# A fused adaLN, Mamba and FFN kernel: the unit numbers of its side work are shifted by one to three

## The chip, the cores and the metric

The kernel runs on one core of one Trainium2 chip. The metric is the device time of one execution in microseconds (us); lower is better. The engines are TensorE (PE in the rows), its weight load (PEld), VectorE (DVE), ScalarE (ACT), GpSimd (POOL) and SyncE (SP), which issues the DMAs.

## The reference, cut to what matters

```python
# x: 16 x 512 x 256; mod = silu(c) @ wmod gives six rows of 256 for each of the 16 sequences
h  = layernorm(x) * (1 + ca) + sa
xn = layernorm(h, ln1);  a = mamba1(xn) + flip(mamba2(flip(xn)))
x  = x + ga * (layernorm(a, ln2) + xn)
h  = layernorm(x) * (1 + cb) + sb
h  = silu(h @ w1) * (h @ w2);  h = gelu(h @ h1);  h = gelu(h @ h2);  x = x + gb * (h @ w3)

# mamba, E = 512 channels, N = 64 states each, T = 512 steps
xp, z = split(xn @ W_in);  xc = silu(conv4(xp) + conv_b)
dt_lo, B, C = split(xc @ W_xp);  dt = softplus(dt_lo @ W_dt + dt_b)
for t: s[e, n] = exp(dt[t, e] * A[e, n]) * s[e, n] + dt[t, e] * xc[t, e] * B[t, n]
y[t, e] = sum_n s[e, n] * C[t, n];   out = ((y + xc * D) * silu(z)) @ W_out
```

All of it is float32; the hidden width of the FFN is 1024.

## The kernel before, in words

Both scans of one sequence are cut into 128 units, numbered 0 to 127. A unit is four groups of 32 channels with four states each on the 128 partitions, times 512 steps, in two halves of 128x1024. For each unit ScalarE makes the decays exp(dt*A) (`decays`, L1083, two units ahead), the driving term dt*x*B comes into PSUM (even units: VectorE multiplies, L1272; odd units: ScalarE and GpSimd make a product `v_sb`, L1096 and L1380, which TensorE transposes into `driven`, L883), VectorE scans each half (L1283), GpSimd multiplies by C (L1313), and TensorE sums over the states into `y_ps` (`accumulate`, L905). There are 4 buffers for states, 2 for the driving term, 2 for `v_sb`.

One body handles one sequence. It also carries side work: the FFN of the sequence before (parts "early" and "late"), the second half of this sequence's projections ("p1"), the output projection ("o0"), and norm and projections of the next sequence ("next"). There are 18 bodies: "pre" (side work alone), "first", fourteen "mid", "last" and "tail" (side work alone).

The order is written out by hand. `side_steps` and `projection_steps` give each step a unit number on each engine, from the constants of L49 to L54; in `body`, each engine does its part of a unit and then the side steps that have this number. Each engine runs its program strictly in order; steps are tied by semaphores. A side result in PSUM has one bank per stream: `p_ps` for projections and `q_ps` for the FFN, and a new TensorE step waits until ScalarE (or VectorE) has taken the step before out of the same bank (`bank_free`, L706). TensorE does the transposes for the odd unit u+1 in unit u, and side steps after them; after the side steps of an odd unit u come at once the transposes for unit u+2.

Names of steps: T, X, K (transpose, input projection, convolution by four matmuls), xc (silu over the convolution), BC, CL, BT (the B and C rows, C again with the low-rank dt, B transposed), D0 to D3, exp, one, rest, ln, dt (softplus), ua, ub (dt*x on GpSimd), cut, Z0 to Z3 and sz (gate and its silu); N, F0 to F7, silu, glu, H0 to H7, gelu, G0 to G7, gelu, W (the FFN; H, G take two units each on TensorE); o_, n_, x_, h_ with stats, aggr (VectorE), rstd (GpSimd), norm (ScalarE); x_scale, x_shift (L1231, L1234), mix (L1238), mixed (L1360). On ScalarE the functions exp, silu, gelu and ln are in different tables, so silu, gelu, ln, xc and sz each sit between two table loads. A unit whose number is in `CROWDED` has more than two TensorE side steps in its pair, and does `accumulate` earlier.

Of the kernel before, what the change touches and what calls it, by code (L numbers as in the profile page):

```python
# [11 lines left out]
BATCH, T, D = 16, 512, 256  # L12
# [6 lines left out]
EC = E // P  # L19
# [28 lines left out]

P1_AT, X_AT, NEXT_AT, O0_AT = 12, 64, 80, 68  # L49
PASS_AT, FIRST_PASS_AT = (3, 5, 7, 9), (118, 119, 120, 121)  # L50
O1_AT, MIX_AT, N_AT, PRE_AT = 3, 15, 24, (5, 7, 14)
FFN_AT = (("early", 26, 38, 55, 72), ("late", 77, 89, 106, 123))
UT_AT = (121, 10, 26, 41, 57, 73, 78, 97)
GAPS = {"p1": 3, "next": 3}  # L54


def projection_steps(part, s):

    gap = GAPS[part]
# [12 lines left out]
    act.append((s + 5, part, "BC", 1))  # L72
    dve.append((s + 6, part, "BC", 1))
    pe += [(s + 7, part, "CL", 0), (s + 8, part, "CL", 1)]
    act.append((s + 8, part, "CL", 2))
    pe += [(s + 9, part, "BT", 0), (s + 10, part, "BT", 1)]
    act.append((s + 10, part, "BT", 1))
    for m in range(EC):
        pe.append((s + 11 + m, part, f"D{m}", 1))
        act.append((s + 11 + m, part, f"D{m}", 2))  # L80
    act += [(s + 15, part, "exp", 1), (s + 15, part, "one", 1)]
    dve.append((s + 17, part, "rest", 2))
    act.append((s + 18, part, "ln", 1))
    dve += [(s + 19, part, "dt", 1), (s + 22, part, "cut", 1)]
    pool = [(s + 20, part, "ua", 1), (s + 21, part, "ub", 1)]
    for m in range(EC):
        pe.append((s + 22 + m, part, f"Z{m}", 1))
        act.append((s + 22 + m, part, f"Z{m}", 1))
    act.append((s + 26, part, "sz", 1))
    return pe, act, dve, pool  # L90


def norm_steps(part, name, s):

    dve = [(s, part, name + "_stats", TT), (s + 1, part, name + "_aggr", TT)]
    if name == "x":
        dve += [(s + 4, part, "x_scale", 1), (s + 5, part, "x_shift", 1)]
    return [(s + 2, part, name + "_rstd", 9)], [(s + 3, part, name + "_norm", TT)], dve


def side_steps():
# [113 lines left out]
def adaln_kernel(nc, x, win, wxp, wdt, wout, f1, h1, h2, w3, cols, rows, c_t, wmod, consts, spread_rows, out):  # L215
    ctx = ExitStack()
    with ctx:
# [239 lines left out]
        def _(sp):  # L457
# [166 lines left out]
            def body(at):  # L624
                for unit in range(UNITS):
# [821 lines left out]
```

## Time and profile before

| | us |
|---|---|
| median of three runs | 12745.45 (12720.19 to 12750.62) |
| the profiled execution | 12767.88, span 12766.1 |
| VectorE busy | 11968.4 (94%) |
| GpSimd busy | 11345.7 (89%) |
| ScalarE busy | 10843.4 (85%) |
| TensorE busy | 10393.6 (81%) |

The span is setup and the body "pre" up to 168 us, sixteen bodies with scans up to 12509 us, and the tail of 257 us. Busy time is the union of an engine's instructions; the idle time printed behind an instruction is that of its engine just before it, with the instruction that ended it. A row of the timeline merges equal instructions that follow each other. The scans of the body that the rows are taken from (the sixth with scans) begin at 4032.7 us and those of the next one at 4799.5 us, so this body is 766.7 us long.

### The profile page before, as it was taken

The page shows a single profiled execution, that of the slowest core. Times are in us where ns is not written, and L with a number is a line of the kernel's source. Part 1 is how long each engine was busy: PE and PEld are TensorE (multiplying, and loading weights), DVE is VectorE, ACT ScalarE, POOL GpSimd, SP SyncE. Part 2 cuts the span into 40 slices and gives each one's busy share as a digit, 9 for nine tenths or more (in the row PEclk, how much of TensorE's full clock was granted, in tenths as well). Part 3 has the DMA queues.
Part 4 walks back from the last instruction along what each step waited for, and adds up shares of the span by engine and source line. Part 5 has one row for each costly group of instructions (what it writes and reads, how often), then busy time and mean ns, then how long its engine had stood idle before and what let it go on. Part 6 is the DMA issues. An engine that isn't in the chain of part 4 may idle for free.

```text
span 12766.1 us, 179504 instructions
## 1 busy us (share of the span) xinstructions
PE 10393.6 (81%) x51484; PEld 5920.3 (46%) x51484; DVE 11968.4 (94%) x7080; ACT 10843.4 (85%) x23460; POOL 11345.7 (89%) x5924
## 2 busy tenths in 40 slices
PE   5678878888888888878888888887878878788887
PEld 2334544445454444544445444454544445444445
DVE  5999999999999999999999999999999999999992
ACT  5788888888888898888888888888888988888882
POOL 4899999899998999999998998999989999999992
PEclk7778988889898998988989898998989989889888
DMA  2223333333333333433333333333333333333332
GB/s 89 83 87 111 119 112 126 122 108 117 110 127 115 117 125 106 130 111 121 122 113 115 112 125 121 109 120 107 128 111 119 123 108 127 112 124 121 111 111 96
DMA packets 610266, 1459.04 MB, mean 114 GB/s; under 512 B 68928, under 2 KB 110032, under 8 KB 604672
## 3 DMA queue, kind: packets, MB, share of 16 engines
q1 hardware_dynamic: 609152, 1446.18, 35.0%
q8 instruction: 456, 7.47, 0.2%
q14 instruction: 658, 5.39, 0.1%
HBM read 1355.09 MB, written 90.83 MB: 113 GB/s over the span
## 4 chain that ended last, share of the span: by engine, by line
issue 26%; PE 25%; ACT 19%; DVE 16%; POOL 10%; DMA 1%; DVEq 0%; POOLq 0%; SPq 0%; ACTq 0%
DVE state L1283 11%; POOL state L1313 8%; PE driven L883 7%; ACT state L1083 7%; ACT v_sb L1096 6%; PE q_ps L838 5%; PE y_ps L905 4%; DVE driven L1272 3%; PE p_ps L746 2%; PE q_ps L825 2%; PE b_ps L873 1%; PE p_ps L754 1%; ACT L1083 1%; PE p_ps L770 1%; PE p_ps L761 1%
## 5 line engine op out<-in xcount | busy, mean ns | idle before, releaser
L1313 POOL TENSOR_TENSOR state<-state,c_rep 128x1024 f32<-128x1024 f32 x4096 | 9682.4, 2393 | 971.5 <-DVE state L1283 965.2
L1283 DVE TENSOR_TENSOR_SCAN state<-state,driven 128x1024 f32<-128x1024 f32 x4096 | 9089.4, 2267 | 298.0 <-PE driven L883 280.5
L1083 ACT ACTIVATE state<-ud_rep,cols_sb 128x512 f32<-128x512 f32 x8192 | 5212.5, 710 | 3.1 <-PE y_ps L905 0.6
L1096 ACT ACTIVATE v_sb<-u_t,b_t 128x128 f32<-128x128 f32 x12288 | 4062.0, 505 | 1136.5 <-PE driven L883 1133.4
L883 PE MATMUL driven<-consts_sb,v_sb 128*128 128x128 f32 x16384 | 2713.9, 320 | 1486.3 <-DVE state L1283 1463.2
L883 PEld LDWEIGHTS driven<-consts_sb,v_sb 128*128 128x128 f32 x16384 | 2184.5, 164 | 2692.0 <-DVE state L1283 2001.2
L905 PE MATMUL y_ps<-state,consts_sb 128*32 128x512 f32 x16384 | 2455.2, 677 | 289.2 <-POOL state L1313 287.1
L1272 DVE TENSOR_TENSOR driven<-ud_rep,b_ps 128x1024 f32<-128x1024 f32 x2048 | 2389.6, 1212 | 18.1 <-DMA ud_rep<-ud_rows 18.1
L838 PE MATMUL q_ps<-hid,wq_sb 128*128 128x256 f32 x7936 | 2081.0, 408 | 139.8 <-ACT hid L1061 76.4
L838 PEld LDWEIGHTS q_ps<-hid,wq_sb 128*128 128x128 f32 x7936 | 1498.0, 199 | 1016.3 <-issue 818.1
L1380 POOL TENSOR_TENSOR v_sb<-u_t,b_t 128x512 f32<-128x512 f32 x1024 | 1083.5, 1058 | 36.4 <-issue 23.5
L905 PEld LDWEIGHTS y_ps<-state,consts_sb 128*32 128x32 f32 x16384 | 346.6, 114 | 1213.9 <-POOL state L1313 675.2
L873 PE MATMUL b_ps<-b_parts,onehot 32*128 32x512 f32 x1024 | 574.2, 561 | 0.0
L825 PE MATMUL q_ps<-xn_q,wq_sb 128*128 128x256 f32 x1984 | 508.6, 400 | 44.9 <-ACT hid L1051 22.4
L746 PE MATMUL p_ps<-x_t,wp_sb 128*128 128x512 f32 x1024 | 503.6, 615 | 37.3 <-ACT xc L989 24.2
L754 PE MATMUL p_ps<-u_pad,dt_sb 128*128 128x512 f32 x1024 | 514.3, 626 | 20.0 <-ACT u_pad L985 19.9
L825 PEld LDWEIGHTS q_ps<-xn_q,wq_sb 128*128 128x128 f32 x1984 | 365.8, 194 | 221.1 <-issue 99.2
L848 PE MATMUL q_ps<-wq_sb,hid 128*128 128x256 f32 x992 | 282.0, 434 | 68.3 <-ACT hid L1066 64.6
L1061 ACT ACTIVATE hid<-q_ps,cols_sb 128x256 f32<-128x256 f32 x496 | 223.4, 450 | 129.7 <-PE q_ps L838 129.5
L746 PEld LDWEIGHTS p_ps<-x_t,wp_sb 128*128 128x128 f32 x1024 | 189.3, 194 | 269.9 <-issue 185.0
L754 PEld LDWEIGHTS p_ps<-u_pad,dt_sb 128*128 128x128 f32 x1024 | 188.1, 197 | 269.2 <-issue 213.7
L873 PEld LDWEIGHTS b_ps<-b_parts,onehot 32*128 32x128 f32 x1024 | 208.5, 204 | 210.4 <-issue 210.4
(141 smaller groups left out, 5585.8 us busy)
## 6 DMA issues: line engine op xcount, KB each, us to landing
c_rep<-bc_rows SPq DMA_DIRECT2D x2048, 256.0 KB, 3.0
ud_rep<-ud_rows SPq DMA_DIRECT2D x512, 512.0 KB, 4.0
wq_sb<-in_h SPq DMA_DIRECT2D x512, 512.0 KB, 3.9
wq_sb<-in_f SPq DMA_DIRECT2D x128, 512.0 KB, 4.2
wp_sb<-in_win SPq DMA_DIRECT2D x64, 512.0 KB, 4.1
dt_sb<-conv_taps SPq DMA_DIRECT2D x32, 1024.0 KB, 5.2
ud_rows<-u_pad SPq DMA_DIRECT2D x128, 256.0 KB, 3.4
ud_rows<-dt_sb SPq DMA_DIRECT2D x128, 256.0 KB, 3.5
```

Source lines behind the costliest of these rows:

```text
L746: mm = pe.matmul(p_ps[:], wp_sb[:, m, k, :], x_t[:, k, :], start=(k == 0), stop=(k == DC - 1))
L825: mm = pe.matmul(bank[:, which * TH:(which + 1) * TH], w[:, m % 2, which, k, :], n_t[:, k, i * TH:(i + 1) * TH], start=(k == 0), stop=(k = ...
L838: mm = pe.matmul(bank[:, 0:TH], w[:, k, :], src[:, k, :], start=(k == 0), stop=(k == HC - 1))
L873: pe.matmul(b_ps[:], onehot[k, g % quarter, :], b_parts[d][k, :], start=True, stop=True).then_inc(b_spread, 1)
L883: mm = pe.transpose(driven[:, q % DRIVE_RING, j % 2, tt * P:(tt + 1) * P], v_sb[:, unit // 2 % V_RING, tt, j].rearrange("p e n -> p (e n)" ...
L905: mm = pe.matmul(y_ps[EG * j:EG * (j + 1), :], over_nn, state[:, k % STATE_RING, j, :], start=False, stop=(g == NG - 1))
L1083: ins = act.activation(state[:, unit % STATE_RING, j, :], ud_rep[:, nth % 2, j, 1, :], ACT.Exp, scale=a_neg[:, d, c, j, g:g + 1])
L1096: ins = act.activation(v_sb[:, unit // 2 % V_RING, tt, :, :, n].rearrange("p j e -> p (j e)"), u_t[:, nth % 2, tt, :], ACT.Identity, scale ...
L1272: dve.tensor_tensor(driven[:, h], u_rows(unit)[:, 2 * h:2 * h + 2], b_ps[:].unsqueeze(1).to_broadcast([P, 2, T]), ALU.mult).then_inc(dve_d ...
L1283: dve.tensor_tensor_scan(flat, flat, driven[:, q % DRIVE_RING].rearrange("p j t -> p (j t)"), 0.0, ALU.mult, ALU.add).then_inc(scanned, 1)
L1313: pool.tensor_tensor(part, part, c_rep[:, unit % ROW_RING, :].unsqueeze(1).to_broadcast([P, 2, T]), ALU.mult).then_inc(was_read, 1)
L1380: pool.tensor_tensor(v_sb[:, unit // 2 % V_RING, TT - 1].rearrange("p j e n -> p (j e) n"), u_t[:, nth % 2, TT - 1, :].unsqueeze(2).to_bro ...
```

## The change

Steps keep their work and their order within each chain; the unit numbers change. The projections of p1 start two units earlier and those of next three earlier; within a projection everything from BC (on VectorE) and CL on comes one unit later relative to its start, rest two, dt, ua, ub, cut and Z three. So in absolute units, before and after: silu of the FFN 34 to 31 and 85 to 83; first gelu 54 to 51 and 105 to 103; second gelu 71 to 69 and 122 to 121; H starts 38 to 35 and 89 to 87; G starts 55 to 53 and 106 to 105; W 72 to 70, and 123 stays. xc 26 to 24 and 94 to 91; D0 34 to 33 and 102 to 100; exp and one 38 to 37 and 106 to 104; rest 40 stays and 108 to 107; dt 42 to 43 and 110 stays; Z0 45 to 46 and 113 stays; sz 49 to 50 and 117 stays. mix goes from 15 to 12, x_norm from 67 to 65, x_scale from 68 to 67. Loads and stores that belong to these steps move with them.

```diff
-P1_AT, X_AT, NEXT_AT, O0_AT = 12, 64, 80, 68
+P1_AT, X_AT, NEXT_AT, O0_AT = 10, 62, 77, 68
-O1_AT, MIX_AT, N_AT, PRE_AT = 3, 15, 24, (5, 7, 14)
-FFN_AT = (("early", 26, 38, 55, 72), ("late", 77, 89, 106, 123))
-UT_AT = (121, 10, 26, 41, 57, 73, 78, 97)
+O1_AT, O_AT, MIX_AT, N_AT, PRE_AT = 3, 7, 12, 21, (5, 7, 10)
+FFN_AT = (("early", 23, 35, 53, 70), ("late", 75, 87, 105, 123))
+UT_AT = (121, 8, 24, 41, 57, 73, 78, 95)
...
-    dve.append((s + 6, part, "BC", 1))
-    pe += [(s + 7, part, "CL", 0), (s + 8, part, "CL", 1)]
-    act.append((s + 8, part, "CL", 2))
-    pe += [(s + 9, part, "BT", 0), (s + 10, part, "BT", 1)]
-    act.append((s + 10, part, "BT", 1))
+    dve.append((s + 7, part, "BC", 1))
+    pe += [(s + 8, part, "CL", 0), (s + 9, part, "CL", 1)]
+    act.append((s + 9, part, "CL", 2))
+    pe += [(s + 10, part, "BT", 0), (s + 11, part, "BT", 1)]
+    act.append((s + 11, part, "BT", 1))
     for m in range(EC):
-        pe.append((s + 11 + m, part, f"D{m}", 1))
-        act.append((s + 11 + m, part, f"D{m}", 2))
-    act += [(s + 15, part, "exp", 1), (s + 15, part, "one", 1)]
-    dve.append((s + 17, part, "rest", 2))
-    act.append((s + 18, part, "ln", 1))
-    dve += [(s + 19, part, "dt", 1), (s + 22, part, "cut", 1)]
-    pool = [(s + 20, part, "ua", 1), (s + 21, part, "ub", 1)]
+        pe.append((s + 12 + m, part, f"D{m}", 1))
+        act.append((s + 12 + m, part, f"D{m}", 2))
+    act += [(s + 16, part, "exp", 1), (s + 16, part, "one", 1)]
+    dve.append((s + 19, part, "rest", 2))
+    act.append((s + 20, part, "ln", 1))
+    dve += [(s + 22, part, "dt", 1), (s + 25, part, "cut", 1)]
+    pool = [(s + 23, part, "ua", 1), (s + 24, part, "ub", 1)]
     for m in range(EC):
-        pe.append((s + 22 + m, part, f"Z{m}", 1))
-        act.append((s + 22 + m, part, f"Z{m}", 1))
-    act.append((s + 26, part, "sz", 1))
+        pe.append((s + 25 + m, part, f"Z{m}", 1))
+        act.append((s + 25 + m, part, f"Z{m}", 1))
+    act.append((s + 29, part, "sz", 1))
...
-        dve += [(s + 4, part, "x_scale", 1), (s + 5, part, "x_shift", 1)]
+        dve += [(s + 5, part, "x_scale", 1), (s + 6, part, "x_shift", 1)]
...
-    for part, name, s in (("early", "o", MIX_AT - 7), ("early", "n", MIX_AT + 3), ("next", "x", X_AT), ("next", "h", X_AT + 7)):
+    for part, name, s in (("early", "o", O_AT), ("early", "n", MIX_AT + 3), ("next", "x", X_AT), ("next", "h", X_AT + 8)):
```

## Rows read from the trace of the kernel before

**Rows 1.** The page's first part: busy time of each engine.

```profile
PE 10393.6 (81%) x51484; PEld 5920.3 (46%) x51484; DVE 11968.4 (94%) x7080; ACT 10843.4 (85%) x23460; POOL 11345.7 (89%) x5924
```

**Rows 2.** Waits of VectorE over the span: total, times, longest, in us.

```profile
DVE state L1283 <- PE driven L883: 280.5, 373, 3.2
```

**Rows 3.** Waits of VectorE in one body, 4033 to 4799 us.

```profile
DVE state L1283 <- PE driven L883: 13.5, 20, 2.0
DVE state L1283 <- ACT state L1083: 2.6, 1, 2.6
...
DVE xa L1231 <- ACT xa L968: 1.1, 1, 1.1
```

**Rows 4.** Waits of VectorE in units 26 to 40 of that body, 4186 to 4283 us.

```profile
DVE state L1283 <- PE driven L883: 3.4, 5, 1.8
DVE b_parts L1249 <- ACT b_parts L997: 2.1, 1, 2.1
```

**Rows 5.** Timeline of TensorE, unit 35: start, us, instruction, [idle before, releaser].

```profile
4248.07 2.07 PE L791 MATMUL p_ps<-sz 16*128 16x512 f32 x2 [4.38 <-ACT u_pad L1015]
4250.07 1.97 PE L883 MATMUL driven<-consts_sb,v_sb 128*128 128x128 f32 x8
```

**Rows 6.** Timeline of ScalarE, units 34 and 35.

```profile
4238.64 2.55 ACT L1083 ACTIVATE state<-ud_rep,cols_sb 128x512 f32<-128x512 f32 x4
4241.09 2.56 ACT L1096 ACTIVATE v_sb<-u_t,b_t 128x128 f32<-128x128 f32 x8
4243.66 1.28 ACT L1055 ACT_TABLE_LOAD   x1
...
4246.77 0.67 ACT L1014 ACTIVATE dt_sb<-p_ps,cols_sb 128x512 f32<-128x512 f32 x1
...
4249.33 2.56 ACT L1083 ACTIVATE state<-ud_rep,cols_sb 128x512 f32<-128x512 f32 x4
```

**Rows 7.** Timeline of TensorE, units 55 to 57.

```profile
4370.75 3.78 PE L838 MATMUL q_ps<-hid,wq_sb 128*128 128x256 f32 x8 [3.31 <-ACT hid L1066]
4374.32 1.92 PE L883 MATMUL driven<-consts_sb,v_sb 128*128 128x128 f32 x8
...
4377.35 1.09 PE L883 MATMUL driven<-consts_sb,v_sb 128*128 128x128 f32 x8
...
4378.80 1.99 PE L838 MATMUL q_ps<-hid,wq_sb 128*128 128x256 f32 x8
```

**Rows 8.** Timeline of TensorE, units 123 and 124.

```profile
4776.52 3.38 PE L848 MATMUL q_ps<-wq_sb,hid 128*128 128x256 f32 x8 [4.84 <-ACT hid L1066]
```

**Rows 9.** Timeline of VectorE, unit 125.

```profile
4780.82 4.46 DVE L1283 TENSOR_TENSOR_SCAN state<-state,driven 128x1024 f32<-128x1024 f32 x2 [1.95 <-PE driven L883]
```

**Rows 10.** Timeline of VectorE, units 106 to 110.

```profile
4662.31 6.63 DVE L1283 TENSOR_TENSOR_SCAN state<-state,driven 128x1024 f32<-128x1024 f32 x3
...
4680.77 2.29 DVE L1253 SCALAR_TENSOR_TENSOR u_pad<-sz,u_pad 128x2048 f32<-128x2048 f32 x1 [2.60 <-ACT sz L1021]
...
4697.19 4.02 DVE L1259 TENSOR_TENSOR dt_sb<-dt_sb,sz 128x2048 f32<-128x2048 f32 x1 [0.80 <-ACT sz L1024]
```

**Rows 11.** Timeline of ScalarE, the steps exp and one and what follows.

```profile
4676.79 1.92 ACT L1018 ACTIVATE u_pad<-u_pad 128x2048 f32<-128x2048 f32 x1
...
4680.65 2.54 ACT L1083 ACTIVATE state<-ud_rep,cols_sb 128x512 f32<-128x512 f32 x4
```

**Rows 12.** Timeline of VectorE, the second half of rest in unit 40.

```profile
4277.96 4.34 DVE L1255 TENSOR_TENSOR dt_sb<-dt_sb,u_pad 128x2048 f32<-128x2048 f32 x1
```

**Rows 13.** Groups of VectorE by line over the span: the step mix.

```profile
L1238 DVE TENSOR_TENSOR o_sb<-o_sb,mod_q 128x1024 f32<-128x1024 f32 x16 | 85.0, 5312 | 5.6 <-ACT o_sb L968 5.6
```

**Rows 14.** Timeline of VectorE, units 118 and 119 and the drive of 120.

```profile
4741.49 8.81 DVE L1283 TENSOR_TENSOR_SCAN state<-state,driven 128x1024 f32<-128x1024 f32 x4
4750.22 2.34 DVE L1272 TENSOR_TENSOR driven<-ud_rep,b_ps 128x1024 f32<-128x1024 f32 x2
```

**Rows 15.** Timeline of ScalarE, the start of unit 118.

```profile
4750.06 2.56 ACT L1083 ACTIVATE state<-ud_rep,cols_sb 128x512 f32<-128x512 f32 x4
```

More of the change, by code:

```diff
@@ L636, in body @@
                         load_pass(at, unit // NG + 1, PASS_AT.index(unit % NG))
-                    if unit == P1_AT + 11 + 3 * GAPS["p1"] and at.has("p1"):
+                    if unit == P1_AT + 12 + 3 * GAPS["p1"] and at.has("p1"):
                         store_bc(at, "p1")
-                    if 0 <= unit - P1_AT - 3 * GAPS["p1"] - 25 < EC and at.has("p1"):
-                        store_ud(at, "p1", unit - P1_AT - 3 * GAPS["p1"] - 25)
-                    if unit == NEXT_AT + 11 + 3 * GAPS["next"] and at.has("next"):
+                    if 0 <= unit - P1_AT - 3 * GAPS["p1"] - 28 < EC and at.has("p1"):
+                        store_ud(at, "p1", unit - P1_AT - 3 * GAPS["p1"] - 28)
+                    if unit == NEXT_AT + 12 + 3 * GAPS["next"] and at.has("next"):
                         store_bc(at, "next")
-                    if 0 <= unit - NEXT_AT - 3 * GAPS["next"] - 25 < EC and at.has("next"):
-                        store_ud(at, "next", unit - NEXT_AT - 3 * GAPS["next"] - 25)
+                    if 0 <= unit - NEXT_AT - 3 * GAPS["next"] - 28 < EC and at.has("next"):
+                        store_ud(at, "next", unit - NEXT_AT - 3 * GAPS["next"] - 28)
                     if unit in FIRST_PASS_AT and at.has("next"):
@@ L660, in body @@
                         load_wxp(at, "next")
-                    if unit == P1_AT + 28 + 3 * GAPS["p1"] and at.has("o0"):
+                    if unit == P1_AT + 31 + 3 * GAPS["p1"] and at.has("o0"):
                         load_wout(at)
```

## The prediction

> **What bounds the kernel now.** I read the busy times first, then the waits of VectorE over the span and in one body, then the timelines of VectorE, TensorE and ScalarE around each of its waits. VectorE is busy 11968.4 of 12766.1 us [rows 1]. Four scans and their two drives make a pair of units: 8.73 us from the first scan to the drives and about 2.25 for these, 10.97 in all, so 4.37 for an even unit and 6.60 for an odd one [rows 14]. The change removes nothing from that; what it can win is VectorE's waits and what its side operations lose. Waits in one body come to 23.5 us of 766.7: 13.5 for TensorE's transposes, 2.6 for the decays, 2.6 for exp and one, 2.1 for BC, 1.1 for x_norm, 0.8 for ln [rows 3, 4, 10] and 0.8 in small pieces. Over the span the first of them is 280.5 us, 17.5 for each of the 16 bodies [rows 2], so this body is a light one, and I scale its TensorE waits by 17.5/13.5 = 1.3.
>
> How such a wait arises is to be seen at the silu of unit 34. ScalarE begins the unit's decays at 4238.64, the product at 4241.09, the silu's table load at 4243.66, and reads D0 out of its bank from 4246.77; it begins unit 35 at 4249.33 [rows 6]. TensorE stands in unit 35 before D1, which wants that bank, for 4.38 us, and then runs the transposes for unit 37 in 1.97 instead of 1.09 us [rows 5, 7]; VectorE waits 1.8 [rows 4]. The first gelu is the same (idle 3.31, then a step of 3.78 instead of 1.99 [rows 7]), and so is the second late gelu (idle 4.84, VectorE waits 1.95 [rows 8, 9]). Two quantities decide: how far ScalarE is behind when the bank is read, and whether the blocked TensorE step has an odd number. After an odd unit's side steps the transposes come at once. TensorE has 10.97 us from the start of odd unit u to the start of u+2, and the transposes take the last 1.1. A blocked step of 2.0 has to start by 7.9 after VectorE began unit u.
>
> ScalarE's cost of a unit, start to start: 2.45 for decays, 2.4 more in even units (4.8 in all), 1.2 in odd ones (3.65), from rows 6 and the short product of four in odd units, which I take as half of the eight. A function of its own with two table loads is 3.1 to its end [rows 6] and 1.28 more, 4.4. Its lag behind VectorE at the start of a unit is the lag at the unit before, plus its cost there, less VectorE's 4.37 or 6.60. At unit 118 it is 4750.06 - 4741.49 = 8.6 us, right after sz [rows 14, 15].
>
> **The change part by part.** All terms are per body.
>
> *Units 23 to 41.* Now VectorE waits 3.4 + 2.1 here [rows 4], scaled 4.4 + 2.1 = 6.5. BC on VectorE gets a unit more behind ScalarE's BC, 4.4 to 6.6 us against a wait of 2.1: gone. After the silu at 31 come BT (two TensorE steps that wait for nothing of it) and D0 in odd unit 33, which waits for BT's reading in ScalarE's unit 32. With a lag of 8.3 (like after sz), less 0.2 or so for the Y step, that is 8.0 after VectorE's 33: D0 takes 1.0, so no wait at full speed and about 1 at half speed. The pairs of units with four long TensorE steps fall from three to one here. I leave 1.7 (0.5 to 3.5): **-4.8**.
>
> *First gelu, early.* G0 gets a free unit, and the wait (1.7, scaled 2.2) goes. But sz moves to unit 50 and the gelu to 51, two functions of 4.4 us side by side. Lag: 8.2 at 51 (as behind the other sz), 8.2 + 3.65 + 4.4 - 6.60 = 9.7 at 52, 10.1 at 53; the decays of unit 55 (first half 1.3 us after ScalarE's 53 starts) are then there at 11.4 against 10.97: 0.4 of wait. G1 in odd unit 55 waits for G0's reading until 7.5: no wait at full speed, 2.2 at half speed. Between them: 1.7 left, **-0.5**.
>
> *Second gelu, late.* It moves from 122 to 121 and W1 stays at 123: the wait of 1.95, scaled 2.5, goes. But G steps now start in odd units. G6 is read in ScalarE's unit 118, straight after sz in 117: lag 8.2 (the 8.6 of rows 15 less one reading), plus 4.8 for the unit and 0.35 for the reading, less 4.37: 8.95 after VectorE's unit 119, where G7 stands. G7 takes 2.0 and the transposes 1.04: 1.0 late at full speed, 3.4 if it takes the 3.78 and 1.92 of rows 7. Idle before it would be 5 us, longer than in any of rows 5, 7 and 8. I take 2.8: **+0.3**.
>
> *xc of next.* It moves from even 94, where H2 was read before it, to odd 91, and H2 is read behind it in 92. The same arithmetic with a lag of 8.3 gives 9.1 after VectorE's 93, where H3 and half of BC stand, 3.7 us: 2.9 late. The silu at 83 does the same to X2 in 85, one step, 0.4 to 3 late, of which GpSimd's backlog behind glu (which holds TensorE back here now) would have cost most anyway. **+2.9** (0 to +5).
>
> *exp, one, rest, ln, dt of next.* VectorE waits 2.60 for one, 0.80 for ln [rows 10]; both go with one more unit of distance. ScalarE's lag behind gelu, D3, exp and one is 4680.65 (its unit 107) less 4666.7 (VectorE's 107: three scans begin at 4662.31, two of them 4.37) = 13.9 [rows 10, 11]. Today VectorE has rest to do (and waits) in 108 before it needs those decays. After the change rest is in 107, three units behind exp and not two: ScalarE is 13.9 late at 105, the first decays of 107 are there 15.2 after VectorE's 105, and it needs them after 10.97. A new wait of 4.3 for the decays, which takes the place of the old one. And rest: in unit 40, without a wait ahead, its second half takes 4.34 [rows 12], against 2.29 for the first after a wait [rows 10]: a GpSimd operation comes between. In 107 I expect a short one, +1.3 (0 to 2.3); dt, which now starts at once after the scans, loses 1.4 of its 4.02. Sum -2.6 - 0.8 - 0.3 + 4.3 + 1.3 - 1.4 = **+0.5** (-3 to +3).
>
> The Trainium skill, SBUF — State Buffer, section Who interferes with whom, says that a VectorE instruction with two SBUF inputs and a GpSimd one that reads SBUF shut each other out for the whole instruction, by order of issue. By that rule, the trace agrees: 4.34 is 2.29 and most of one GpSimd operation.
>
> *x_norm, x_scale, x_shift.* The wait of 1.1 goes [rows 3]; x_scale then starts straight behind the drives with GpSimd busy, which costs it 0 to 2.1, the difference in rest; I take 0.9: **-0.2**. *mix* takes 5.3 on average [rows 13] and stays among GpSimd's operations, as rstd and pre2 now follow each other: **0** (-2 to +2). BC at 28, ua, ub and Z one later, loads: **+0.5** for the pairs 46 to 49, now both of four long steps. The DMAs move with their steps, each still a unit or more ahead of its reader: 0. Pre and tail keep their order on every engine: 0. The 2.6 at the start of a body stays.
>
> Sum: -4.8 - 0.5 + 0.3 + 2.9 + 0.5 - 0.2 + 0 + 0.5 = -1.3 per body, times 16 (first and last carry part of the steps) -21 us. On the profiled 12767.9 that is 12747. The median stands 22 lower than the profiled run, so **12725**.
>
> The Trainium skill, ScalarE: Activation LUTs, section What ACT_TABLE_LOAD costs, adds a drain of 1.38 us to each load. The trace differs: the load starts 0.01 behind the product before it [rows 6], and no term here has a drain.
>
> **The rivals.** A, *faster*: ScalarE is a little less behind, and the steps in 93 and 119 are not blocked past the limit. For it: both exceed it by 1 us or so at full speed, and each lag is my estimate. Against: the half speed after idling. It takes away 2.9 and 2.8: -7.0 per body, -112, 12633.
>
> B, *slower*: TensorE's half speed follows each new idle stretch. The rows show it behind 3.31, 4.38 and 4.84 us [rows 5, 7, 8]: about the double of 1.99 and 1.09, as at the lower of the clock's two levels (1.2 and 2.4 GHz). At 33, 55, 85, 93 and 119 a step of 2.0 and the transposes take 2.6 longer; 13 in all, of which about 6 are in the sum: +5.7 net, +91 over 16, 12836. [...]
>
> C, *slower*: GpSimd's operations come between mix, x_scale, x_shift, rest and dt more often: 5 of them at 2.05 (4.34 - 2.29) less the 2.2 counted and the 1.4 taken off for dt is +9.4, but not all meet one; half of that is +4.7, net +3.4: 12799.
>
> D, *it does nothing*: all silu and gelu waits only move to the next odd unit, body by body the same 23.5: 12745. That is near my forecast, and held with it.
>
> **How the numbers follow.** Forecast with D 0.40; A 0.33; B 0.17; C 0.10. A measurement of this kernel can tell about 0.3% (38 us) from no change, so faster is below 12707, slower above 12784. Faster: A and a little of the forecast's spread, 0.38. Slower: B and most of C, 0.24. Same: 0.38. The single terms go from -6 to +5 per body, which together give about 4 per body, 65 us, around 12725; the range goes to A below and B above, 12620 to 12840.
>
> **What would show it.** Right: VectorE's wait for BC near 0, its wait for one at L1253 gone, and a new wait of the scans for the decays of 3 to 5 us per body near unit 107; TensorE idle before H3 (unit 93) and before G7 (119) and VectorE waiting behind it; no wait at 125. Wrong: no wait for the decays at 107 (then ScalarE's lag is overrated and A holds), or idle TensorE at 33, 55 and 85 followed by half speed (B), or x_scale and rest above 4 us each (C).

## The result and the profile after

The changed kernel takes 12817.7 us (median, 12814.4 to 12819.0) against 12746.6 for the kernel before: ratio 1.006, 95% interval 1.0042 to 1.0077. It is slower by 71 us. The forecast was 12725, 21 us less than before; the measured time lies inside the range, but it moved the other way, and it ends 18 us from rival B's 12836.

The profiled execution has a span of 12814.7 us, 48.6 more than before. Its busy times, to be held against [rows 1]:

```profile
PE 10278.8 (80%) x51484; PEld 5854.4 (46%) x51484; DVE 11913.4 (93%) x7080; ACT 10888.8 (85%) x23460; POOL 11417.0 (89%) x5924
```

VectorE is busy 55 us less than before, and the span is 49 longer: it waits 104 us more. The waits of VectorE over the span (total us, times, longest):

```profile
DVE state L1283 <- PE driven L883: 359.3, 305, 5.7
DVE state L1283 <- ACT state L1083: 87.9, 44, 4.3
```

The first answers to [rows 2], 280.5 us there in 373 pieces: fewer waits, but longer ones. The second was 10.2. The same in one body, 4045 to 4823 us, against [rows 3]:

```profile
DVE state L1283 <- PE driven L883: 24.2, 18, 4.0
DVE state L1283 <- ACT state L1083: 6.2, 3, 4.3
DVE xc L1202 <- PE y_ps L905: 1.6, 2, 1.4
DVE dt_sb L1262 <- POOL u_pad L1368: 1.1, 1, 1.1
```

The waits for u_pad (exp and one), b_parts, xa and dt_sb <- ACT of [rows 3, 4, 10] are gone from the body, as forecast: 6.6 us. In their place stand 10.7 more for TensorE's transposes and 3.6 more for the decays.

What TensorE waited for shows it best: three of its groups over the span, busy us, mean ns | idle before them, and by whom ended. These are of the kernel before:

```profile
L838 PE MATMUL q_ps<-hid,wq_sb 128*128 128x256 f32 x7936 | 2081.0, 408 | 139.8 <-ACT hid L1061 76.4 <-ACT hid L1066 53.9 <-POOL hid L1364 8.9
L825 PE MATMUL q_ps<-xn_q,wq_sb 128*128 128x256 f32 x1984 | 508.6, 400 | 44.9 <-ACT hid L1051 22.4 <-DMA wq_sb<-in_f 21.4 <-ACT xn_q L1042 0.9
L746 PE MATMUL p_ps<-x_t,wp_sb 128*128 128x512 f32 x1024 | 503.6, 615 | 37.3 <-ACT xc L989 24.2 <-ACT sz L1029 10.8 <-ACT u_pad L1015 1.4
```

and these of the changed one:

```profile
L838 PE MATMUL q_ps<-hid,wq_sb 128*128 128x256 f32 x7936 | 2048.9, 403 | 316.6 <-ACT hid L1061 301.7 <-POOL hid L1364 8.9 <-ACT hid L1066 5.4
L825 PE MATMUL q_ps<-xn_q,wq_sb 128*128 128x256 f32 x1984 | 534.1, 416 | 92.8 <-ACT hid L1051 53.3 <-DMA wq_sb<-in_f 37.7 <-ACT xn_q L1042 0.9
L746 PE MATMUL p_ps<-x_t,wp_sb 128*128 128x512 f32 x1024 | 532.1, 645 | 76.3 <-ACT xc L989 63.4 <-ACT sz L1029 10.6 <-ACT u_pad L1015 1.4
```

L838 are the steps H and G, L825 the steps F, L746 the steps X and Z. L1066 is gelu itself: the free unit behind it works, 53.9 us fall to 5.4. L1061, L1051 and L989 are the short copies with which ScalarE empties TensorE's bank. The waits for those rise by 225, 31 and 39 us. The functions' time has not gone; it stands ahead of the next copy.

By stretches of units, the mean of bodies 1 to 14 in us, worked out from the starts of the first scans of the units in the two traces, against the terms of the sum:

| units | forecast | measured | what it is |
|---|---|---|---|
| 0-19 | 0 | -2.4 | mix -3.4, a new wait of 0.9 at 15 |
| 20-41 | -4.8 | -0.4 | BC gone; new waits 2.1 at 31, 2.3 + 1.4 at 35 |
| 42-49 | +0.5 | +1.0 | cut waits 1.1 for GpSimd's ub |
| 50-57 | -0.5 | +0.4 | decays 1.9 at 54 and 55 in place of 2.0 at 57 |
| 58-73 | -0.2 | -2.1 | x_norm's wait and small ones gone |
| 74-81 | 0 | +4.7 | 3.5 at 77, 1.4 at 80 |
| 82-91 | 0 | +1.9 | 3.7 at 87, less 2.2 at 91 |
| 92-103 | +2.9 | +1.8 | 3.4 at 95, less small ones |
| 104-115 | +0.5 | -0.3 | 4.2 for the decays at 107 in place of 2.6 + 0.8 |
| 116-127 | +0.3 | -0.5 | 3.0 at 121 in place of 2.7 at 125 |
| sum | -1.3 | +4.0 | |

4.0 in each of 14 bodies is 56 us; the first and last body and what lies around them give 7 back.

In the names of the FFN's steps the first digit is 0 for early and 1 for late: H13 is the prediction's H3, G17 its G7, and F06 is the seventh F step of early.

A mean over the bodies hides one thing. One and the same step, behind the same idle time, runs at full speed in some bodies of one execution and wholly or partly at half speed in others. F06 in unit 29 with the step behind it, in the body from 4045 us and in the one from 5601, both of the changed kernel:

```profile
4221.67 2.85 PE L825 MATMUL q_ps<-xn_q,wq_sb 128*128 128x256 f32 x8 [2.12 <-ACT hid L1051]
4224.31 2.76 PE L761 MATMUL p_ps<-xc,sz 128*80 128x512 f32 x4
...
5776.85 1.99 PE L825 MATMUL q_ps<-xn_q,wq_sb 128*128 128x256 f32 x8 [2.13 <-ACT hid L1051]
5778.67 1.88 PE L761 MATMUL p_ps<-xc,sz 128*80 128x512 f32 x4
```

The granted clock is 0.66 from 4222 to 4227 us and 1.00 from 5777.7 to 5782.6. VectorE's wait at unit 31 is 2.4 us behind the first pair and 0.7 behind the second. It is 2.4 in 11 of the 14 bodies here, and in 0 to 8 of 14 in the other kernels with these units. H13 in unit 93, in the body from 4045 us and in the next:

```profile
4616.39 1.99 PE L838 MATMUL q_ps<-hid,wq_sb 128*128 128x256 f32 x8 [3.07 <-ACT hid L1061]
...
5392.22 2.62 PE L838 MATMUL q_ps<-hid,wq_sb 128*128 128x256 f32 x8 [3.07 <-ACT hid L1061]
```

The wait at 95 is 2.9 behind the first kind, in 11 bodies, and 4.6 to 5.7 behind the second, in three. In the kernel before, the wait at 91 is 1.4 or 3.0 in the same way, behind an H step of 1.99 or of 3.5 to 3.7 us in unit 89. So a difference of about 1 us per body between two kernels at 31, 91 or 95 can come from the number of bodies at half speed, with no edit near it; below such differences are named. No run tests what chooses between the two.

### The profile page after: what moved, and what is told of

Read it like the earlier page. It is cut to its first block, busy times and chain, and to the rows that moved or that the text cites. A ratio compares the mean times of both kernels' runs of the same rounds, so it can differ in the third digit from the quotient of the medians.

```text
span 12814.7 us, 179504 instructions
## 1 busy us (share of the span) xinstructions
PE 10278.8 (80%) x51484; PEld 5854.4 (46%) x51484; DVE 11913.4 (93%) x7080; ACT 10888.8 (85%) x23460; POOL 11417.0 (89%) x5924
## 4 chain that ended last, share of the span: by engine, by line
PE 26%; issue 23%; ACT 22%; DVE 14%; POOL 11%; DMA 1%; DVEq 0%; SPq 0%; POOLq 0%; ACTq 0%
DVE state L1283 10%; POOL state L1313 9%; ACT state L1083 8%; PE driven L883 8%; ACT v_sb L1096 7%; PE q_ps L838 5%; PE y_ps L905 4%; DVE driven L1272 3%; PE p_ps L746 2%; PE q_ps L825 2%; ACT L1083 1%; PE b_ps L873 1%; PE p_ps L754 1%; DMA wq_sb<-in_f 1%; PE p_ps L761 1%
## 5 line engine op out<-in xcount | busy, mean ns | idle before, releaser
L883 PE MATMUL driven<-consts_sb,v_sb 128*128 128x128 f32 x16384 | 2655.7, 316 | 1473.3 <-DVE state L1283 1456.6
L883 PEld LDWEIGHTS driven<-consts_sb,v_sb 128*128 128x128 f32 x16384 | 2152.9, 162 | 2696.3 <-DVE state L1283 1893.9
L838 PE MATMUL q_ps<-hid,wq_sb 128*128 128x256 f32 x7936 | 2048.9, 403 | 316.6 <-ACT hid L1061 301.7
L838 PEld LDWEIGHTS q_ps<-hid,wq_sb 128*128 128x128 f32 x7936 | 1473.5, 195 | 1209.0 <-issue 1007.4
L1380 POOL TENSOR_TENSOR v_sb<-u_t,b_t 128x512 f32<-128x512 f32 x1024 | 1151.2, 1124 | 36.2 <-issue 23.1
L825 PE MATMUL q_ps<-xn_q,wq_sb 128*128 128x256 f32 x1984 | 534.1, 416 | 92.8 <-ACT hid L1051 53.3
L746 PE MATMUL p_ps<-x_t,wp_sb 128*128 128x512 f32 x1024 | 532.1, 645 | 76.3 <-ACT xc L989 63.4
L825 PEld LDWEIGHTS q_ps<-xn_q,wq_sb 128*128 128x128 f32 x1984 | 381.3, 202 | 287.0 <-issue 156.5
L1061 ACT ACTIVATE hid<-q_ps,cols_sb 128x256 f32<-128x256 f32 x496 | 226.1, 456 | 130.8 <-PE q_ps L838 130.6
L746 PEld LDWEIGHTS p_ps<-x_t,wp_sb 128*128 128x128 f32 x1024 | 198.9, 203 | 300.8 <-issue 190.4
L1051 ACT ACTIVATE hid<-q_ps,cols_sb 128x256 f32<-128x256 f32 x496 | 202.4, 462 | 99.2 <-PE q_ps L825 99.1
```

Source lines behind the costliest of these rows:

```text
L746: mm = pe.matmul(p_ps[:], wp_sb[:, m, k, :], x_t[:, k, :], start=(k == 0), stop=(k == DC - 1))
L825: mm = pe.matmul(bank[:, which * TH:(which + 1) * TH], w[:, m % 2, which, k, :], n_t[:, k, i * TH:(i + 1) * TH], start=(k == 0), stop=(k = ...
L838: mm = pe.matmul(bank[:, 0:TH], w[:, k, :], src[:, k, :], start=(k == 0), stop=(k == HC - 1))
L883: mm = pe.transpose(driven[:, q % DRIVE_RING, j % 2, tt * P:(tt + 1) * P], v_sb[:, unit // 2 % V_RING, tt, j].rearrange("p e n -> p (e n)" ...
L1380: pool.tensor_tensor(v_sb[:, unit // 2 % V_RING, TT - 1].rearrange("p j e n -> p (j e) n"), u_t[:, nth % 2, TT - 1, :].unsqueeze(2).to_bro ...
```

## The experiments

Ratios are to the kernel before, with their 95% interval; waits are means per body over bodies 1 to 14.

### Which half loses, and what mix is worth

The part of mix alone, on the kernel before:

```diff
-O1_AT, MIX_AT, N_AT, PRE_AT = 3, 15, 24, (5, 7, 14)
+O1_AT, O_AT, MIX_AT, N_AT, PRE_AT = 3, 7, 12, 24, (5, 7, 10)
...
-    for part, name, s in (("early", "o", MIX_AT - 7), ("early", "n", MIX_AT + 3), ("next", "x", X_AT), ("next", "h", X_AT + 7)):
+    for part, name, s in (("early", "o", O_AT), ("early", "n", MIX_AT + 3), ("next", "x", X_AT), ("next", "h", X_AT + 7)):
```

> The kernel before with one part of the change alone: the attention norm at 7, mix at 12, pre2 at 10, the norm n behind mix; all else as before. Theory: mix takes 5.6 us in unit 15 because GpSimd operations that are queued there come before it (pre2 at 14 and a backlog of products); at 12 it takes 2.2, as in the changed kernel. That is -3.4 per body, -54 over 16 bodies: 12692, ratio 0.9958. Rival: the gain of mix belongs to its new neighbours in the changed kernel (projection started two units earlier), here it stays at 5 us: 12746, ratio 1.000.

Measured: 12716.3, ratio 0.9974 (0.9962 to 0.9985). The group of mix in this kernel, against [rows 13]:

```profile
L1238 DVE TENSOR_TENSOR o_sb<-o_sb,mod_q 128x1024 f32<-128x1024 f32 x16 | 31.6, 1977 | 5.6 <-ACT o_sb L968 5.6
```

2.0 us and not 5.3, so the gain needs nothing else of the change; the changed kernel has 2114 ns in the same group. The bodies are 3.3 shorter on average. The run moves mix, the norm o and pre2 together and does not tell which of GpSimd's operations cost mix its time. (The Trainium skill, SBUF — State Buffer, section Who interferes with whom, lets a VectorE instruction with two SBUF inputs and a reading GpSimd one shut each other out by order of issue; a mix of 5.3 us at one place and 2.0 at another agrees with that.) From one profiled execution to the other the span fell by 55 us, as forecast, but the median by 30: the profiled execution of the kernel before stands 21 us above its median, this one 3 below. No row tells where the typical execution loses the rest.

Units 62 to 127 as before, the rest changed:

```diff
-P1_AT, X_AT, NEXT_AT, O0_AT = 10, 62, 77, 68
+P1_AT, X_AT, NEXT_AT, O0_AT = 10, 64, 80, 68
-FFN_AT = (("early", 23, 35, 53, 70), ("late", 75, 87, 105, 123))
+FFN_AT = (("early", 23, 35, 53, 70), ("late", 77, 89, 106, 123))
...
+    w = 1 if part == "p1" else 0
...
+    act += [(s + 15 + w, part, "exp", 1), (s + 15 + w, part, "one", 1)]
+    dve.append((s + 17 + 2 * w, part, "rest", 2))
```

> The changed kernel with units 62 to 127 as before (norms at 64 and 71, projection of next at 80 with the old distances, late FFN at 77, 89, 106, UT7 at 97); the early half stays changed. Theory: the early half is worth -1.5 per body (mix -3.4, BC and first gelu gone, new stalls at 31 and 35) and the late half is the loser: waits at 77, 80, 87, 95, 107 and 121 vanish, those of before at 91, 108 and 125 return: -5.6 per body, 12817 - 84 = 12733, ratio 0.999. Rival: the early half is the loser by its stalls in 31 and 35 and mix gains nothing lasting: ratio above 1.003, 12785 or more.

Measured: 12677.2, ratio 0.995 (0.9934 to 0.9967). The early half of the change makes the kernel faster by 69 us, and the late half costs 140 on top of it, not the 84 that were forecast. In its trace the waits of VectorE for TensorE are 222.8 us, and TensorE's group L838 waits 163.7 and not 316.6. The theory's split was right in its main point, that the late half is the loser; the early half won 69 us and not 24. Part of the difference is the clock and not the order of work: the wait at 31 is 0.7 in all 14 bodies, where the changed kernel has 2.4 in 11, and the waits that came back at 91 and 125 are 1.4 and 1.8, where the kernel before has means of 2.2 and 2.7.

### The wait at unit 77: a load that passed another

The forecast had nothing here. TensorE in the changed kernel, unit 76 on (start, us, instruction, [idle before, releaser]):

```profile
4502.45 1.90 PE L905 MATMUL y_ps<-state,consts_sb 128*32 128x512 f32 x8 [3.13 <-POOL state L1313]
4506.75 3.78 PE L825 MATMUL q_ps<-xn_q,wq_sb 128*128 128x256 f32 x8 [2.40 <-DMA wq_sb<-in_f]
4510.32 1.91 PE L883 MATMUL driven<-consts_sb,v_sb 128*128 128x128 f32 x8
```

F10 waits for its weights, and the DMA queue says why. The queue in the changed kernel, and below it in the kernel before:

```profile
4498.12 0.51 SPq L511 DMA_DIRECT2D dt_sb<-conv_taps  x1
4498.82 0.81 SPq L543 DMA_DIRECT2D wq_sb<-in_f  x2
```

```profile
4496.94 0.80 SPq L543 DMA_DIRECT2D wq_sb<-in_f  x2
4500.16 0.54 SPq L553 DMA_DIRECT2D c_rep<-bc_rows  x1
4500.84 0.50 SPq L511 DMA_DIRECT2D dt_sb<-conv_taps  x1
```

The load of the convolution taps (1 MB) hangs on NEXT_AT, which moved by three units; the chunks of F hang on the late FFN, which moved by two. Both stood in unit 76, chunks first; now the taps are in 73 and the chunks in 74, behind them. The edit puts them into one unit again:

```diff
-                    if unit == NEXT_AT - 4 and at.has("next"):
+                    if unit == NEXT_AT - 3 and at.has("next"):
                         load_conv(at, "next")
```

> The changed kernel with the load of next's convolution taps (1 MB) one unit later in the DMA queue, so that the first two weight chunks of the late FFN are issued ahead of it in unit 74 and not behind it. Theory: TensorE's wait of 2.4 us for the first chunk before step F10 and the half-speed step behind it are from this order; VectorE's wait at unit 77 falls from 3.5 to at most 1, and the 1.35 at unit 80 to about 0.8: -3 per body, -45 over 15 bodies: 12772, ratio to the kernel before 1.002. Rival: the accumulate in unit 76 that waits for GpSimd (3.1 us idle) sets it, not the DMA: the wait at 77 stays at 3 or more, 12817, ratio 1.0056.

Measured: 12755.7, ratio 1.0002 (0.999 to 1.0014). The same steps in this kernel:

```profile
4474.02 1.93 PE L905 MATMUL y_ps<-state,consts_sb 128*32 128x512 f32 x8 [3.13 <-POOL state L1313]
4475.88 2.67 PE L825 MATMUL q_ps<-xn_q,wq_sb 128*128 128x256 f32 x8
4478.39 1.04 PE L883 MATMUL driven<-consts_sb,v_sb 128*128 128x128 f32 x8
```

The idle time for GpSimd is the same 3.13, the one for the DMA is gone, and VectorE's wait at 77 goes from 3.5 to 0.25. So the rival falls. One line of the queue's order is worth 62 us, nearly the whole loss. Not all of it is in unit 77: 1.0 less at 31 and 1.4 more at 95 came with it. The steps there and the idle time before them are the same; half speed stands at 31 in 3 bodies and not in 11, and at 95 in 11 and not in 3. Together the two all but cancel out.

### The steps behind a function

Three waits come from a step of TensorE in an odd unit that needs a bank which ScalarE empties only behind a function. First sz, one unit later:

```diff
-    act.append((s + 29, part, "sz", 1))
+    act.append((s + (29 if part == "p1" else 30), part, "sz", 1))
```

> The changed kernel with one function one unit later: the silu of z for next in 118, behind G16's reading, not in 117 ahead of it. Theory: the step G17 in odd unit 119 waits for G16's reading only because that stands behind sz; VectorE's wait of 3.0 at unit 121 falls below 0.5: -2.7 per body, -41: 12777, ratio 1.0024. Rival: the block moves to the next reading: G17 is read in 120 behind sz and gelu at 121 comes late, so a wait of 2 to 3 us appears at 123 or 125: 12817, ratio 1.0056.

Measured: 12765.7, ratio 1.0012 (0.9998 to 1.0027). G17 in the changed kernel stood idle and was slow:

```profile
4778.22 3.02 PE L838 MATMUL q_ps<-hid,wq_sb 128*128 128x256 f32 x8 [4.11 <-ACT hid L1061]
4781.03 1.73 PE L883 MATMUL driven<-consts_sb,v_sb 128*128 128x128 f32 x8
```

With sz behind the reading, the 3.0 at 121 are gone and nothing of over 0.2 follows up to 125. The theory holds. The 52 us are 11 more than forecast; the wait at 31 is 1.1 lower (half speed in 2 bodies), which this edit does not touch, and the one at 95 0.6 higher.

Then xc from 91 to 92 and BC one later. UT7 (TensorE transposes dt*x of the eighth pass into the same bank, ScalarE copies it out) goes to 96, or BC and UT7 lock each other out:

```diff
-    act.append((s + 3, part, "xc", 1))
+    w = 1 if part == "next" else 0
+    act.append((s + 3 + w, part, "xc", 1))
...
-UT_AT = (121, 8, 24, 41, 57, 73, 78, 95)
+UT_AT = (121, 8, 24, 41, 57, 73, 78, 96)
```

> The changed kernel with the silu xc of next in unit 92, behind H12's reading, and BC (TensorE 93 and 94, ScalarE 94, VectorE 96) and UT7 (96) one later with it. Theory: H13 in odd unit 93 waited only because H12's reading stood behind xc, so VectorE's wait at unit 95 (3.4 us in the changed kernel) falls to about 0.5 (BC's first half in 93 still waits a little for xc): -2.9 per body, -44: 12774, ratio 1.0022; the wait of 4.2 for the decays at 107 stays. Rival: the block moves with xc, BC in 93 now waits for it in full, and the wait at 95 stays at 3 or more: 12817, ratio 1.0056.

Measured: 12776.7, ratio 1.0027 (1.0016 to 1.0038). The wait at 95 is gone, 3.4 to below 0.1, but 1.7 came back at 99. The time was as forecast, 12774, but with luck: without the 1.0 less at 31 (half speed in 3 bodies and not in 11) it would have been about 16 us more.

X2 and what follows one later as well:

```diff
-        x = s + 2 + gap * m
+        x = s + 2 + gap * m + (1 if part == "next" and m > 1 else 0)
```

> As the run with xc in 92, and X2, K2, X3, K3 of next each one unit later, so that the odd unit 85 behind the silu of 83 has no step that waits for a reading (X2 stands in even 86). Theory: the 3.7 us at unit 87 are X2's wait for K1's reading behind that silu, and the half-speed step and transposes behind the idle time; they fall below 0.7: together with xc -6 per body, -90: 12727, ratio 0.9985. Rival: GpSimd's backlog behind the two glu products in 84 and 85 sets the accumulate and the transposes there anyway (that wait was 2.2 at unit 91 in the kernel before): 2 us or more stay at 87, 12750 or more, ratio 1.0003.

Measured: 12807.0, ratio 1.0049 (1.0032 to 1.0066), 80 us above the forecast. The 3.7 at 87 fell to 1.3, so they did belong to X2; but in small pieces all of it returned: 1.3 at 89 to 93 (two long steps in each pair of units there), 0.8 more at 99, 1.5 more at 112, where the Y step (VectorE's product of the summed y, L1202) waits for TensorE. Neither theory holds: below 0.7 or 2 us and more had been forecast for unit 87.

D0 to D3 of p1 one later:

```diff
-        pe.append((s + 12 + m, part, f"D{m}", 1))
-        act.append((s + 12 + m, part, f"D{m}", 2))
+        d = s + 12 + m + (1 if part == "p1" else 0)
+        pe.append((d, part, f"D{m}", 1))
+        act.append((d, part, f"D{m}", 2))
```

> The changed kernel with D0 to D3 of p1 one unit later (34 to 37), so that the odd unit 33 behind the silu of 31 has no step. Theory: D0 in 33 waited for BT's reading behind the silu and then ran at half speed; VectorE's waits at 35 (2.3 + 1.4) vanish: -3.2 per body over 16 bodies, -50: 12767, ratio 1.0016. Rival: the four-step units 35 and 37 (D1 with H00, D3 with H01) and exp and one straight behind D3's reading bring a wait of 2 or more at 37 or for the decays at 39: ratio 1.004 or more.

Measured: 12790.6, ratio 1.0037 (1.0023 to 1.0051), 24 us above the forecast. The first wait at 35 is gone, 0.9 of the second is left, and 2.2 stand at 37: the rival's wait at its place, if with a little less of a loss. TensorE there:

```profile
4239.53 1.94 PE L906 MATMUL y_ps<-state,consts_sb 128*32 128x512 f32 x8 [2.44 <-POOL state L1314]
4241.40 3.78 PE L839 MATMUL q_ps<-hid,wq_sb 128*128 128x256 f32 x8
4245.11 1.42 PE L792 MATMUL p_ps<-sz 16*128 16x512 f32 x2
```

No step waits for a bank here. The first H step takes 3.78 us and not 1.99, behind 2.44 us of idle time for GpSimd's product and an `accumulate` of 1.94.

### Lateness or half speed

At 85 and 33 of the changed kernel, X2 and D0:

```profile
4568.56 3.78 PE L746 MATMUL p_ps<-x_t,wp_sb 128*128 128x512 f32 x4 [4.36 <-ACT xc L989]
4572.13 1.91 PE L883 MATMUL driven<-consts_sb,v_sb 128*128 128x128 f32 x8
...
4249.05 2.07 PE L791 MATMUL p_ps<-sz 16*128 16x512 f32 x2 [4.57 <-ACT b_t L1006]
4251.05 1.97 PE L883 MATMUL driven<-consts_sb,v_sb 128*128 128x128 f32 x8
4252.95 1.94 PE L905 MATMUL y_ps<-state,consts_sb 128*32 128x512 f32 x8
4254.81 1.97 PE L883 MATMUL driven<-consts_sb,v_sb 128*128 128x128 f32 x8
```

The table of stretches has the granted clock (stretch, us, TensorE's busy time, clock, DMA share, GB/s), first with the idle time, then X2:

```profile
4562.00:4568.00 6.00, 2.20 (x11) 0.95 0.15 44
4568.00:4574.00 6.00, 5.44 (x16) 0.50 0.41 131
```

0.50 is the lower of the two levels, 1.2 of 2.4 GHz. To tell this from the lateness, extra matmuls fill the gap and nothing else moves:

```diff
+WARM = {33: ("early", "F07"), 85: ("late", "F17")}
...
+                if unit in WARM and at.has("late") and at.has("next" if unit > 64 else "p1"):
+                    pe.wait_ge(act_side.sem, act_side.done(at, *WARM[unit]))
+                    for _ in range(12):
+                        pe.matmul(q_ps[:, 0:TH], ident, n_t[:, 0, 0:TH], start=True, stop=True)
```

> The changed kernel with nothing moved; in units 33 and 85, where TensorE stands idle before D0 and X2 (4.6 and 4.4 us), 12 extra matmuls of 128x256 are put ahead of the waiting step, about 3.0 us at full speed, whose result nobody reads. It tells the half speed behind idle time from the lateness itself. Theory (half speed is most of these waits): D0 and X2 run in 1.1 and 2.0 us in place of 2.1 and 3.8, the transposes behind them in 1.1 in place of 1.9; VectorE's wait at 87 falls from 3.7 to 1.1, at 35 from 3.7 to about 0.7: -5.6 per body, -88: 12729, ratio 0.9987. Rival (only ScalarE's lateness counts): both waits stay, 12817 or more by the extra work, ratio 1.0056.

Measured: 12788.1, ratio 1.0029 (1.0015 to 1.0043), 30 us less than without them and 59 above the forecast. Unit 85 in this kernel:

```profile
4544.09 5.45 PE L857 MATMUL q_ps<-xn_q,consts_sb 128*128 128x256 f32 x24
4549.37 1.88 PE L747 MATMUL p_ps<-x_t,wp_sb 128*128 128x512 f32 x4
4551.09 1.04 PE L888 MATMUL driven<-consts_sb,v_sb 128*128 128x128 f32 x8
```

and its clock:

```profile
4544.00:4549.00 5.00, 5.00 (x27) 1.00 0.09 33
4549.00:4553.00 4.00, 4.00 (x23) 1.00 0.59 196
```

The fill took 5.45 us and not the 3.0 that I had reckoned. Each of these matmuls is two records: four of an H step are x8 and 1.99 us in the rows above, and these 12 are x24. X2 so starts 0.8 us later than without them, measured from VectorE's unit 85; still the wait at 87 falls from 3.7 to 2.1, and at 35 from 3.7 to 1.3 (with 1.1 at 37, 0.4 before). X2 and the transposes are through in 2.8 us and not 5.5. In the body shown the wait of the changed kernel is 4.0: 2.7 of it were half speed and 1.2 lateness, and with the late start of 0.8 that is the 2.1 left. The waits at 35, 37 and 87 are 3.2 us less in all. At 95, which was not filled, 1.2 came back (half speed in 13 bodies and not in 3).

### The decays at 107

```diff
-    act += [(s + 16, part, "exp", 1), (s + 16, part, "one", 1)]
+    act += [(s + 16, part, "exp", 1), (s + 16 + (part == "next"), part, "one", 1)]
```

> The changed kernel with one of next in unit 105, behind that unit's decays and products, not in 104 with exp. Theory: the decays of unit 107 wait because gelu (103), D3, exp and one stand ahead of ScalarE's unit 105; without one's 1.9 us the wait falls from 4.2 to 2.3 and nothing new comes before rest: -1.9 per body, -29: 12788, ratio 1.003. Rival: rest in 107 now waits for one, the same 1.9 at another place: 12817, ratio 1.0056.

Measured: 12781.5, ratio 1.0027 (1.0014 to 1.004). VectorE at 107 in this kernel:

```profile
4664.61 4.46 DVE L1283 TENSOR_TENSOR_SCAN state<-state,driven 128x1024 f32<-128x1024 f32 x2 [2.24 <-ACT state L1083]
4668.99 2.34 DVE L1272 TENSOR_TENSOR driven<-ud_rep,b_ps 128x1024 f32<-128x1024 f32 x2
4671.23 2.57 DVE L1253 SCALAR_TENSOR_TENSOR u_pad<-sz,u_pad 128x2048 f32<-128x2048 f32 x1
```

The wait is less by 2.1 on average, the 1.9 of one and a little, and rest follows the drives with no wait. The forecast of this wait held in size and place. That the time came so near as well (12788 forecast) is partly luck: 1.1 more at 112, where the Y step waits for TensorE, stand against 0.9 less at 31, half speed in 4 bodies and not in 11.

### Together

The edits to the taps' load, sz, xc, X2 and D0 of p1 in one kernel:

> The changed kernel with all single edits: taps' load behind the weight chunks, sz of next in 118, xc in 92, X2 in 86, D0 to D3 of p1 in 34 to 37. Theory: the waits are separate, so the gains add: 3.0 + 3.0 + 6.0 + 3.2 = 15 per body, -230 over 15 to 16 bodies: 12588, ratio 0.9876, faster than both kernels. Rival: with each wait that goes ScalarE and GpSimd are further behind at the next place and give a third of it back: 12660, ratio 0.993.

Measured: 12692.2, ratio 0.996 (0.9946 to 0.9975), above even the rival's number. 15 us per body had been forecast, 8.8 were gained. The largest return is at unit 99:

```profile
4581.80 2.85 PE L763 MATMUL p_ps<-xc,sz 128*80 128x512 f32 x4 [1.99 <-ACT u_t L1040]
4584.44 1.86 PE L904 MATMUL y_ps<-xc,skip_w 128*128 128x512 f32 x2
```

CL waits for the bank that UT7 has filled in the same unit, and is slow behind the idle time. UT7 therefore goes to a unit of its own, with D0 to D3 of next behind it:

```diff
-UT_AT = (121, 8, 24, 41, 57, 73, 78, 96)
+UT_AT = (121, 8, 24, 41, 57, 73, 78, 100)
...
-        d = s + 12 + m + (1 if part == "p1" else 0)
+        d = s + 12 + m + 1
```

> The kernel of the five edits with UT7 not in 96, where CL waits behind ScalarE's copy of it, but in unit 100 alone, and D0 to D3 of next in 101 to 104. Theory: the 3.2 us at unit 99 are a bank wait of CL made by the edit to xc; they go, the wait of 4.2 for the decays at 107 stays: 12692 - 46 = 12646, ratio 0.992. Rival: D3's step and reading in 104 right at exp and one make ScalarE later, so the decays wait 5 or more at 107 and a new stall comes at 105: 12692, ratio 0.996.

Measured: 12648.3, ratio 0.9919 (0.9888 to 0.995), two us from the forecast. The 3.2 at 99 are gone, the decays wait 4.5 at 107, and 1.2 stand at 112. Its waits over the span, in the slowest of its four executions (12673.2):

```profile
DVE state L1285 <- PE driven L885: 180.1, 316, 3.1
DVE state L1285 <- ACT state L1085: 92.7, 56, 4.7
```

This is the fastest of all. With D0 of p1 back in 33 and the extra matmuls:

> As the run with UT7 in 100, but D0 to D3 of p1 stay in 33 to 36 and the 12 extra matmuls stand in units 33 and 85. Theory of half speed: the waits at 35 and 37 (0.9 + 1.9 with D0 in 34) fall to 0.7, and the 1.0 at 87 to 0: 12646 - 40 = 12606, ratio 0.989. Rival: they come back, 12646 or more, ratio 0.992.

Measured: 12656.0, ratio 0.9926 (0.9902 to 0.9949), no gain. The waits at 35 and 37 are 1.3 and 1.1 in place of 0.9 and 1.9, and those at 87 to 89 stay near 1.5, where 0 had been forecast. That the fill is too long to be worth its own time is my reading; no run has a shorter one.

## Why the prediction was wrong

**What bounds the kernel, and how a wait arises**: right. VectorE is the bound, and the rule of the first part (how late ScalarE reads the bank, and whether the blocked step is odd) foretold the new waits at 95 (2.9 forecast, 3.4 measured, and 2.9 in the 11 bodies with H13 at full speed), 107 (4.3, 4.2) and 121 (2.8, 3.0; its bound of 3.4 for half speed is 3.7 by its own terms, and three bodies have 3.8), and that those at 57, 108, 110 and 125 go. The runs with sz in 118, xc in 92 and one in 105 show the cause of each. rest and dt were forecast at +1.3 and -1.4: rest takes 2.58 + 3.01 in place of 2.29 + 2.29, dt 2.57 in place of 4.01.

**Units 23 to 41**: -4.8 forecast and -0.4 measured. The step that failed was "that is 8.0 after VectorE's 33: D0 takes 1.0, so no wait at full speed and about 1 at half speed". First, the lag. For G7 the prediction adds 4.8 for ScalarE's unit and 0.35 for the reading and takes off VectorE's 4.37; for D0 it left this out. With it the same lag of 8.3 less 0.2 gives 8.9, which is just the limit for a step of 1.0 (10.97 - 1.1 - 1.0). The trace has D0 at 9.5 in all 14 bodies, 0.6 too late even at full speed. Second, half speed was taken for D0 alone. It lasts over D0, the transposes, the accumulate and the second transposes, 7.7 us where full speed is 4.2 (the same four in the run with the filled gap), and so there are two waits, 2.3 and 1.4. Third, the wait at 31 was left out: F06 in odd 29 waits for F05's reading and starts 7.2 after VectorE's 29, and with CL's step behind it that is too late by 0.7 at full speed and by 2.4 at half speed.

**X2 in unit 85** was named, "0.4 to 3 late", and not given a term of its own, since it was to take the place of GpSimd's backlog. It did take away the 2.2 at 91, but it cost 3.7: 1.2 of lateness and the rest half speed, as the run with the filled gap shows.

**"The DMAs move with their steps, each still a unit or more ahead of its reader: 0"** failed. It looked at each load and its reader and not at the order of two loads: the taps passed the chunks, and F10's 512 KB came behind 1 MB. That is 3.5 us per body at 77, and 62 us in the measured time. It is the largest single error, a term put at nothing; with the order mended the changed kernel is no slower than before.

**mix**, 0 (-2 to +2): it gained 3.4, outside its bounds. It was taken to stay among GpSimd's operations; the run with mix alone shows that its time depends on its unit and on what GpSimd does there.

**First gelu**: the wait for the decays at 55 is 0.4, as forecast, but 1.5 stand at 54 (sz in 50 and gelu in 51 side by side); the half speed of G1, 2.2 in the bounds, did not come. The sum was off by 0.9 only. **x_norm**: 1.1 of wait went. x_scale takes 1.62 and not 2.35, but x_shift behind it 2.33 and not 1.52, so the two together stay as they were; the rest is small waits around them: -2.1 and not -0.2.

**The rivals.** B was nearest. It named 33, 55, 85, 93 and 119 as places of half speed. 33, 85 and 119 have it in all bodies, 93 in 3 of 14, and 55, behind only 1.3 us of idle time, in none. A fell: the steps in 93 and 119 start 9.4 and 9.3 after VectorE's unit, past the limit of 7.9. C fell: mix and dt lost 3.4 and 1.4 us, against which rest and x_shift gained 1.0 and 0.8 and x_scale lost 0.7. D fell, since the waits grew.

**The sum** was off by 5.3 per body. Three errors (20 to 41 by 4.4, 74 to 81 by 4.7, 82 to 91 by 1.9) less three gains (0 to 19 by 2.4, 58 to 73 by 1.9, 92 to 103 by 1.1) make up nearly all of it. Over the span of the two profiled executions that is 49 us more where 21 less were forecast, 70 in all. The other 22 of the 93 between 12725 and 12817.7 are no matter of the change: the forecast took off the 22 us by which the profiled execution of before stands above the median, and the profiled execution of the changed kernel stands 1 us below its own. The sum also scaled the waits by 1.3 from a light body. That body is the shortest of the fourteen, with a granted clock of 0.92.

**What stays open**: what makes F06 run at half speed in 11 bodies of one kernel and in none of another that has the same steps there, behind the same 2.1 us of idle time; and whether the adjacent sz and gelu at 50 and 51 could be parted with a gain.

## What to carry to other kernels

When two groups of side work move by different numbers of units, write down the order of each shared queue before and after, the DMA queue first: one load that passes another can cost as much as everything else in the change. A free unit behind a function on ScalarE does not remove its time; find the next copy that TensorE's bank waits for, and see whether the function stands ahead of it. Count a stretch of idle TensorE not by its length but with the steps at half speed behind it, up to the next transposes that VectorE needs. And before a difference of one wait between two kernels is put down to an edit, look at that wait in each body: if it has two values, count them.

## What was not expected of the hardware

Half speed came behind shorter idle stretches than [rows 5, 7, 8] show: 3.78 for 1.99 us behind 3.13 and 2.40 us with a step between, and behind 2.44 us in the run with D0 in 34; and it lasted over four groups at D0. But the length of the idle stretch does not decide alone. In the run with the taps' load behind the chunks, the same step F10 took 2.67 us behind 3.13 us of idle time and one slow step, with the transposes after it at full speed, 1.04; and in the changed kernel 2.12 us of idle time before F06 bring half speed in 11 of 14 bodies, 3.07 before H13 in 3.

The same program does not have bodies of the same length. In the kernel with mix alone they are 772 to 775 us up to the sixth after the first and then 765.2 to 768.2 to the end, 768.0 to 768.2 in most, with the same order of work. The long ones lose 1.3 to 2.1 us at each of the units 90, 114, 124 and 127 and win 1.1 and 1.2 at 71 and 78, mostly in waits for TensorE. The granted clock goes with it: the G step of unit 112 takes 3.78 us in the long body from 4025 us (at 4709.06) and 1.99 in the short one from 7877 (at 8559.16), in both with no idle time of over 0.4 us just ahead of it. The kernel before has bodies of 767 to 779 us; the shortest and the longest (stretch, us, TensorE's busy time, clock, DMA share, GB/s):

```profile
4032.70:4799.50 766.80, 630.30 (x3212) 0.92 0.37 118
6341.60:7120.80 779.20, 652.65 (x3224) 0.89 0.36 117
```

The kernel with the late half undone has 767.5 to 768.4 in all after the first. So two kernels can differ by several us per body in which steps meet the lower level, and that is as much as most of the single edits here are worth. No run tested what chooses the length.
